# Second edge pass of a graph network: node sums over three edge tiles in two rounded matmul passes, run four steps behind instead of one

## The reference, cut to what matters

```python
x = layernorm(x + relu(gcn(x)))          # first layer: sums over edges into dst
# second layer, for each edge e = (i = src, j = dst):
xs, xv = x[:, :128] @ Ws, x[:, 128:] (128 x 3 values per node) @ Wv
s2, v2 = products of xs[j], xv[j] and the unit vector Y(e)
W  = (softplus-MLP of 20 edge features) * edge_weight
agg = segment_sum(concat(s2, v2) * W, i)
S, V = agg @ W1_s ..., agg @ W1_v @ W2_v
x = layernorm(x + concat(softplus(S) @ W2_s, V))
```

## Time and profile before

| | us |
|---|---|
| three runs, median (lowest, highest) | 1123.79 (1123.58, 1126.42) |
| the profiled execution, its own time | 1128.47 |
| its span in the profile | 1126.6 |
| PE busy, share of the span | 957.1 (85%) |
| DVE busy | 805.6 (72%) |
| ACT busy | 643.7 (57%) |
| POOL busy | 592.5 (53%) |
| mean granted TensorE clock | 0.897 of 2.4 GHz |

### The profile page before, as it was taken

How to read it: one execution, slowest core, us unless ns; L and a number is a source line. 1 busy time by engine, 2 the same in 40 slices (tenths; PEclk the granted TensorE clock), 3 DMA queues, 4 the chain that set the end, 5 groups by cost and what they waited for, 6 DMA issues and landing times.

```text
span 1126.6 us, 17245 instructions
## 1 busy us (share of the span) xinstructions
PE 957.1 (85%) x4727; PEld 739.9 (66%) x4727; DVE 805.6 (72%) x2527; ACT 643.7 (57%) x1460; POOL 592.5 (53%) x683
## 2 busy tenths in 40 slices
PE   6789999999848999999995699999999999444443
PEld 6768777877636888777774477777777777233332
DVE  7888877877716877877876466666666666278887
ACT  1169877877732555555555244445444444178887
POOL 3328888888742666666664456665665664300000
PEclk9979998999888999999998799999999999855555
DMA  9979999999995999999997588888888887599994
GB/s 353 419 249 233 246 241 238 259 240 246 224 235 178 307 324 316 311 313 313 313 315 265 170 184 202 194 204 205 194 201 205 197 198 150 101 354 363 368 347 169
DMA packets 152119, 285.77 MB, mean 254 GB/s; under 512 B 17690, under 2 KB 53950, under 8 KB 152030
## 3 DMA queue, kind: packets, MB, share of 16 engines
q1 hardware_dynamic: 103534, 191.44, 49.1%
q0 software_dynamic: 35392, 82.86, 37.0%
q10 hardware_dynamic: 13104, 10.43, 2.8%
HBM read 137.56 MB, written 147.10 MB: 253 GB/s over the span
## 4 chain that ended last, share of the span: by engine, by line
PE 37%; ACT 12%; issue 9%; DVE 8%; DMA 3%; ACTq 2%; POOL 1%; DVEq 0%; SPq 0%; POOLq 0%
PE bank L1175 6%; PE bank L1186 5%; PE bank L1143 4%; ACT node_mem L663 4%; DVE node_mem L916 3%; PE bank L1184 3%; PE bank L1200 3%; PE bank L1198 3%; PE bank L1201 3%; PE bank L1168 2%; ACT G_hi L646 2%; PE bank L1147 2%; PE bank L1182 2%; PE bank L1176 2%; ACTq L647 2%
## 5 line engine op out<-in xcount | busy, mean ns | idle before, releaser
L545 POOL DMA_INDIRECT sum<-R_mem,l_sidx x79 | 125.8, 1592 | 129.3 <-ACT R_mem L675 79.1
L489 POOL DMA_INDIRECT sum<-R_mem,sidx_all x79 | 128.9, 1632 | 73.2 <-DVE sidx_all L867 35.6
L520 POOL TENSOR_TENSOR node_mem<-node_mem,G_mem 128x512 f32<-128x512 f32 x75 | 96.9, 1292 | 87.9 <-ACT node_mem L657 87.8
L1143 PE MATMUL bank<-W0h,G_hi 128*128 128x512 f32 x316 | 132.3, 419 | 0.4 <-ACT G_hi L646 0.2
L1143 PE MATMUL bank<-W0l,G_hi 128*128 128x512 f32 x316 | 124.3, 393 | 0.0
L657 ACT ACTIVATE node_mem<-node_mem 128x512 f32<-128x512 f32 x75 | 47.5, 633 | 112.3 <-DVE node_mem L916 112.3
L965 DVE SCALAR_TENSOR_TENSOR edge_mem<-edge_mem,Y,bank 128x128 f32<-128x128 f32 x237 | 71.9, 387 | 49.8 <-ACT edge_mem L693 49.2
L693 ACT COPY edge_mem<-bank 128x256 f32<-128x256 f32 x79 | 29.4, 372 | 134.9 <-PE bank L1186 133.2
L1068 PE MATMUL bank<-G_hi,M_mem 128*128 128x512 f32 x200 | 89.0, 445 | 11.7 <-ACT R_mem L589 11.6
L1215 PE MATMUL bank<-ident,node_mem 128*128 128x128 f32 x80 | 27.5, 448 | 82.0 <-DVE node_mem L994 81.9
L537 POOL DMA_INDIRECT G_mem<-x_d,dst_i x79 | 78.3, 992 | 32.6 <-issue 30.7
(11 more groups left out here) (181 smaller groups left out, 2746.9 us busy)
## 6 DMA issues: line engine op xcount, KB each, us to landing
filt_d<-node_mem SPq DMA_DIRECT2D x40, 512.0 KB
G_mem<-x SPq DMA_DIRECT2D x79, 256.0 KB, 4.2
node_mem<-sum SPq DMA_DIRECT2D x79, 256.0 KB, 4.0
x_d<-node_mem SPq DMA_DIRECT2D x79, 256.0 KB, 2.5
node_mem<-filt_d SPq DMA_DIRECT2D x79, 256.0 KB
sum<-zeros SPq DMA_DIRECT2D x33, 512.0 KB
sum<-node_mem SPq DMA_DIRECT2D x79, 192.0 KB, 3.5
edge_mem<-sum SPq DMA_DIRECT2D x15, 512.0 KB, 5.2
```

The costliest lines, as they stand in the source:

```text
L489: pool.indirect_dma_start(sum0, bass.IndirectOffsetOnAxis(ap=sidx[:, t:t + 1], axis=0), R[t % 8][:, :], None, compute_op=ALU.add).then_inc ...
L520: pool.tensor_tensor(res[a], res[a], xl[a], ALU.add).then_inc(n_sum, 1)
L545: pool.indirect_dma_start(sum1, bass.IndirectOffsetOnAxis(ap=l1_sidx[:, t:t + 1], axis=0), R3[t % 8][:, :], None, compute_op=ALU.add).then ...
L1143: pe.matmul(bank[4 + a][:, :], zT_hi[a][:, c * P:(c + 1) * P], w[:, c, :], start=(c == 0 and w is W0h), stop=False)
```

## The change

Three tiles form a group now, where two did. For the tile with place j in its group there are j+1 blocks of the sum, of 128 sources each. The message times the edge's weight is split into two fp32r (rounded fp32) parts, `msg_hi` from ACT and `msg_lo` from DVE, each block is multiplied by both, and `M3` is 0/1 without the weight. So a group has 6 x 2 = 12 sum matmuls of fp32r operands; they accumulate in banks 4, 7 and 1 over three steps. The tile whose sums run in step s is s-10 (it was s-7), and they stand ahead of the second weights. The fifth transpose goes into columns 256 to 384 of `bank[5]`, since bank 1 now holds a sum. `us` runs in ACT's step s for tile s-7 (it was s-6). On DVE the messages, now those of tile s-7, come before the products of tile s-5. For tiles below 60 the trash rows are still counted in the first stage, with three index rows a step where there were four; for the last 19 DVE counts them in `edges1`.

```diff
-        M3 = ring("M3", 4, [P, 2 * P])
+        M3 = [[M_mem.rearrange("p a b -> p (a b)")[:, (6 * i + j * (j + 1) // 2) * P:(6 * i + (j + 1) * (j + 2) // 2) * P]
+               for j in range(3)] for i in range(3)]
+        msg_hi, msg_lo = G_hi, G_lo
...
+        sum_bank = (4, 7, 1)
...
 # SP
-                sp_.dma_start(trow3[g % 4][:, :], src_row[:, g * 256:(g + 1) * 256].broadcast_to([P, 256])) \
+                w = min(384, NP - g * 384)
+                sp_.dma_start(trow3[g % 4][:, 0:w], src_row[:, g * 384:g * 384 + w].broadcast_to([P, w])) \
...
 # POOL, r = g - 5
-                        pool.wait_ge(f_scat, 32 * r)
-                    for t in range(2 * r, min(2 * r + 2, TR)):
+                        pool.wait_ge(f_scat, 48 * r)
+                    if 3 * r >= LATE:
+                        pool.wait_ge(w_sidx, 2 + 2 * (r - T4 + 1))
+                    for t in range(3 * r, min(3 * r + 3, TR)):
...
 # ACT, e = s - 11
+                if live(s, 7):
+                    t, a = s - 7, (u - 7) % 4
+                    act.wait_ge(f_o, t + 1)
+                    wait(act, f_lo, t - 3)
+                    act.copy(msg[a][:, 0:256], bank[5][:, 0:256]).then_inc(f_us, 1)
                 if live(s, 4):
...
+                    act.copy(rawT[b][:, 512:640], bank[5][:, 256:384]).then_inc(f_rawT, 1)
                     act.copy(rawT[b][:, 0:512], bank[0][:, :]).then_inc(f_rawT, 1)
-                    act.copy(rawT[b][:, 512:640], bank[1][:, 0:P]).then_inc(f_rawT, 1)
+                if live(e, 0) and e % 3 == 2:
+                    for t in range(e - 2, e + 1):
+                        sums_out(t)
...
+                if live(s, 8):
+                    act.wait_ge(f_msg, K_MSG * (t + 1))
...
+                    act.activation(msg_hi[a][:, :], msg[a % 4][:, P:640], ACT.Identity, scale=ew[:, t:t + 1]).then_inc(f_hi, 1)
...
 # DVE, tm = s - 9
-                    dve.tensor_scalar(M3[c % 4][:, 0:w], trow3[r][:, 0:w], src_f[:, bass.ds(tm, 1)], ew[:, bass.ds(tm, 1)],
-                                      ALU.is_equal, ALU.mult).then_inc(f_M, 1)
+                    dve.tensor_scalar(M3[gm % 3][jm], trow3[gm % 4][:, 0:wm], src_f[:, tm:tm + 1], None, ALU.is_equal) \
+                       .then_inc(f_M, 1)
...
+                if live(s, 9):
+                    dve.wait_ge(f_hi, tm + 1)
+                    dve.scalar_tensor_tensor(msg_lo[tm % 8][:, :], msg[tm % 4][:, P:640], ew[:, tm:tm + 1],
+                                             msg_hi[tm % 8][:, :].bitcast(F32), ALU.mult, ALU.subtract).then_inc(f_lo, 1)
+                    if tm >= LATE:
...
+                        dve.scalar_tensor_tensor(trow[tm % 2][:, 0:wm], M3[gm % 3][jm].bitcast(F32), 1.0, before[:, Q - wm:Q],
+                                                 ALU.mult, ALU.mult, accum_out=l1_dup[:, tm:tm + 1]).then_inc(w_dup, 1)
+                        if jm == 2 or tm == TR - 1:
...
+                            sums_to(3 * gm, tm + 1, 2 + 2 * (gm - T4))
...
 # PE, the fifth transpose of tile t = s - 4, then the sums
-                    pe.transpose(bank[1][:, 0:P], G3[a][:, 0:C], ident[:, :]).then_inc(f_tr, 1)
+                    wait(pe, f_us, t - 2)
+                    pe.transpose(bank[5][:, 256:384], G3[a][:, 0:C], ident[:, :]).then_inc(f_tr, 1)
...
+                if live(s, 10):
+                    t = s - 10
+                    g, j = t // 3, t % 3
+                    last = j == 2 or t == TR - 1
+                    pe.wait_ge(f_lo, t + 1)
+                    pe.wait_ge(f_M, t + 1)
+                    for k in range(j + 1):
+                        if k == j:
+                            wait(pe, f_ev, 3 * g - 2 + k)
+                        for part_ in (msg_hi, msg_lo):
+                            ins = pe.matmul(bank[sum_bank[k]][:, :], M3[g % 3][j][:, k * P:(k + 1) * P], part_[t % 8][:, :],
...
                 if live(s, 6):
...
+                    pe.wait_ge(f_rawT, 2 * min(t + 2, TR - 1) + 1)
```

More of the change, by code:

```diff
@@ L25 @@
 NR = TR * P
+G1 = (TR + 2) // 3
+LATE = 3 * T4
 Q = 4 * P
@@ L304, in build @@
         f_msg = sem("f_msg")
+        f_hi = sem("f_hi")
+        f_lo = sem("f_lo")
         f_M = sem("f_M")
@@ L529, in _ @@
             pool.wait_ge(w_sidx, 2)
-            for g in range(T2 + 5):
-                if g < T2:
-                    for t in range(2 * g, min(2 * g + 2, TR)):
+            for g in range(G1 + 5):
+                if g < G1:
+                    for t in range(3 * g, min(3 * g + 3, TR)):
                         if t >= 8:
@@ L669, in edges1, with sums_out @@
             def edges1(s, u):
[L670 to L682, removed]
+                e = s - 11
+                def sums_out(t):
+                    act.wait_ge(f_mm, t + 1)
+                    wait(act, f_scat, 48 * (t // 3 - 1))
+                    act.copy(R3[t % 8][:, :], bank[sum_bank[t % 3]][:, :]).then_inc(f_ev, 1)
+                if live(s, 7):
[3 more added lines that the diff above has]
+                    act.copy(msg[a][:, 0:256], bank[5][:, 0:256]).then_inc(f_us, 1)
                 if live(s, 4):
@@ L701, in edges1 @@
                                    scale=Y[:, bass.ds(t, 1), 0]).then_inc(f_proj0, 1)
-            for s in range(TR + 8):
+            for s in range(TR + 11):
                 edges1(s, s % 8)
@@ L820, in counts1 @@
                     if s >= 1:
[L821 to L826, removed]
+                        dve.wait_ge(w_dup, 3 * s)
+                    for v in range(3):
+                        t, w = 3 * s + v, (v + 1) * P
+                        dve.scalar_tensor_tensor(junk1[v][:, 0:w], bank[3][:, 0:w], src_f[:, t:t + 1], before[:, Q - w:Q],
+                                                 ALU.is_equal, ALU.mult, accum_out=l1_dup[:, t:t + 1]).then_inc(w_dup, 1)
                 if s >= 1:
@@ L944, in edges1 @@
                                                      ALU.mult, ALU.add))
+                if live(s, 7):
+                    t, c = s - 7, (u - 7) % 4
+                    dve.wait_ge(f_us, t + 1)
+                    st = Stage(f_msg, t, K_MSG)
+                    mo = msg[c][:, 256:640].rearrange("p (c i) -> p c i", i=3)
+                    for i in range(3):
+                        st.mark(dve.scalar_tensor_tensor(mo[:, :, i], msg[c][:, 0:P], Y[:, bass.ds(t, 1), i],
+                                                         bank[6][:, i * P:(i + 1) * P], ALU.mult, ALU.add))
                 if live(s, 5):
@@ L1047, in _, with index_rows @@
             pe.wait_ge(s_wTc, 3)
[L1049 to L1051 removed]
+            def index_rows(cols, to, g, n=4):
+                for v in range(n):
+                    t = n * g + v
                     ins = pe.transpose(to[:, v * P:(v + 1) * P], cols[:, t:t + 1].broadcast_to([P, P]), ident[:, :])
@@ L1176, in edges1 @@
                     pe.matmul(bank[3][:, 0:P], Wins[:, :], rawT[b][:, 512:640], start=True, stop=True).then_inc(f_wv, 1)
+                if live(s, 10):
[9 more added lines that the diff above has]
+                            ins = pe.matmul(bank[sum_bank[k]][:, :], M3[g % 3][j][:, k * P:(k + 1) * P], part_[t % 8][:, :],
+                                            start=(k == j and part_ is msg_hi), stop=(last and part_ is msg_lo))
+                        if last:
+                            ins.then_inc(f_mm, 1)
                 if live(s, 6):
@@ L1188, in edges1 @@
                     ins.then_inc(f_o, 1)
[L1189 to L1200, removed]
-                        pe.matmul(bank[7][:, :], M3[a][:, P:2 * P], msg[a][:, P:640], start=True, stop=True).then_inc(f_mm, 1)
-            for s in range(TR + 7):
+            for s in range(TR + 10):
                 edges1(s, s % 8)
```

63 lines of the change are left out of this document (31 added, 32 removed).

## The result

| | before | after |
|---|---|---|
| median of four runs, us | 1124.20 | 1136.98 |
| lowest, highest | 1123.58, 1126.42 | 1136.08, 1139.16 |
| profiled execution, its span | 1126.6 | 1137.4 |

The ratio is 1.0101, 95% interval [1.0083, 1.0119]: 12.8 us slower. The forecast was 1135.8 us, 12.0 slower.

What follows compares the result with a forecast made beforehand. PE's array time was taken to bound the second edge pass; steady steps +6.9, beginning -3.7, steps 83 and 84 +1.3, way out +7.5, index rows +0.5 and first pass -0.5 gave +12.0, 1135.8 us, range 1119 to 1149.

Steps and rivals of the forecast that it cites:

- The pause at the fifth transpose: Second edge pass: PE's fifth transpose waits for ACT's `us` copy from the same bank, 0.29 us in every step.
- A: PE's five transposes in a step: 0.55 us before, forecast to end 0.84 after the previous second weights.
- The pause at the bank: Second edge pass: a group's first sum waits until ACT empties bank 4, 0.51 us once in three steps.
- B: PE's first weights in a step: 1.08 us, forecast to end 1.92 after the previous second weights.
- The three kinds of step: Second edge pass: steps with two, four and six sum matmuls take 4.23, 4.19 and 4.65 us, mean 4.36.
- ACT and DVE at nothing: Second edge pass: ACT (4.22 us in its longest step) and DVE (3.6 a step) keep PE's pace, costing nothing.
- The beginning and steps 83 and 84: Second edge pass: steps 7 to 9 without sums save 3.7 us; the last two steps cost 1.3 more.
- The way out: From the last second weights to the last stage's loads: scatter-add rounds take 24.1 us, not 16.6, +7.5.
- First edge pass and index rows: Fewer index transposes and counts in the first edge pass, -0.5 us; more first index rows ahead of the gathers, +0.5.
- No pauses: Rival, second edge pass: PE's waits are covered, a step takes 3.90 us, total 1101; chance 0.15.
- Only one pause: Rival, second edge pass: only `us` is waited for; PE steps 3.72, 4.19, 4.65, ACT gives 0.3 back, 1129; chance 0.14.
- The clock did not fall: Rival, second edge pass: PE's pauses lower its granted clock to 0.93, +21 us, total 1157; chance 0.10.

Runs made afterwards that it cites:

- the second pair: The kernel before and the changed kernel, both unaltered, run again on one other chip: 1128.71 and 1142.69 us, ratio 1.0107.
- both edits: Changed kernel with the fifth transpose moved to bank 3 and ACT's copy of the group's first sum moved ahead of `us`: 1107.74 us, 0.978 of before.
- the second experiment: Changed kernel with only ACT's copy of the group's first sum moved ahead of `us`: 0.9965 of before.

## Why the prediction was right

- **What bounds.** PE's array time, with pauses added to it. Right: with the pauses taken away one at a time the steps fell by 0.24 each and 0.57 once in three, with both by 1.32 for three, and half the sum matmuls brought 1.25 to 1.35.
- **The pause at the fifth transpose.** Forecast A = 0.84, measured 0.79. The handover from PE to ACT (0.20) and the copy (0.37) were as in the earlier trace rows; the restart was over-priced. I took 0.16 beyond the array time from a 512-column fp32r matmul; at this transpose it is 784.23 - 784.01 - 0.11 = 0.11.
- **The pause at the bank.** Forecast PE's restart at 2.43 after the last second weights, measured 790.74 - 0.23 - 788.06 = 2.45. Its removal brought 0.57 of a step, where 0.51 stood, because A was shorter and so B ended sooner. That the restart came out to 0.02 hides two errors: the copy ended at 2.23 and not 2.27 (789.69, 0.60 long), and PE's restart behind it took 0.22 and not the 0.16 of the earlier trace rows.
- **The three kinds of step.** Forecast 4.23, 4.19, 4.65; measured 4.25, 4.16, 4.62. Per step +0.07 instead of +0.095, hence +4.8 instead of +6.9 over 73 steps.
- **ACT and DVE at nothing.** Right in the changed kernel: PE's waits for DVE are 0.7 us in all from 640 to 975 us. ACT's step with three sums ends so that `us` begins 0.20 after the second weights each time.
- **The beginning and steps 83 and 84.** -3.7 and +1.3 forecast, -3.9 (-2.9 in the second pair) and +1.1 measured.
- **The way out** is the term that was mis-sized: +7.5 forecast, +10.0 and +11.3 measured. The mechanism was right, three rounds from about the end of the last second weights. But the round of 72 to 74 started at +2.5 and not +1.3, since the landing before it took 4.51, and the two landings that I put at 3.8 and 3.77, the shorter of those in the earlier trace rows, took 4.62 and 4.28. With 5.0, the other row, the sum would have been nearer. The upper bound of the tail, +3 or 10.5 in all, held the first measurement and was passed by 0.8 in the second.
- **First edge pass and index rows.** -0.5 and +0.5 forecast; the start of the pass moved by -1.7 in one pair of traces and by 0.0 in the other, and the spread between traces is larger than either term, so neither is confirmed. The second is also not what its source gives: 0.25 MB at 292 GB/s are 0.9 us.
- **The rivals.** "No pauses" (1101) did not occur in the changed kernel, but describes the kernel with both edits, whose way out (23.6) is near the 24.1 that the rival took: 0.978 x 1124.2 is 1099.5. "Only one pause" has the steps of the second experiment (3.72, 4.19 and 4.65 for 3.68, 4.15 and 4.62), but neither ACT's 0.3 nor the way out of 24.1 came, so 1120.3 and not 1129. DVE did not set the pace. The clock did not fall: 1.00 from 660 to 965 us with two kinds of pause in it. By the Trainium skill, page TensorE: Matmul & The Clock Gate, section on PSUM-queue depth-cycling, it could have swung; pauses of 0.24 and 0.57 us did not bring that about here. The sum matmuls of 512 columns keep the array for 0.23 each (785.56 to 785.79, and 3.90 a step without gaps bears it out). The 131 ns that the same page of the Trainium skill gives, in its section "Back-to-back issue gap", found no support here; the measured 0.23 decides.

That the total was met to 1.2 us is in part luck. Two errors of opposite sign nearly cancel, 2.1 to 2.5 us too much for the steps and 2.5 to 3.8 too little for the way out, and the two pairs of traces themselves differ by 2.6 (10.8 and 13.4 between the spans).

## What to carry to other kernels

When work is moved away from between a result and the next use of its buffer, write down for each engine what now lies over the handover, in us: here 0.44 of transposes over a handover of 0.68 (0.20, the copy's 0.37, 0.11), where at least 0.86 of sums had lain over it as well. Look for a free piece of another bank and for the place of the copy in the other engine's list before giving up the saving; two small edits turned +1.0% into -2.2%. And price the drain by itself: a chain of transfers that wait for one another is hidden in the steady pass and bare at its end. Larger groups lengthened it here by 10 to 11 us, and an earlier copy out of the first bank, which lets each round start earlier, took 3 to 4 back.

## What the runs showed that I had not expected

- The restart after a wait costs less for a 128-column transpose (0.11 from the end of ACT's copy beyond the array time) than for a 512-column fp32r matmul (0.16 in the earlier trace rows, 0.22 at the bank in the second edge pass).
- The list of waits can miss a pause: PE shows none at L1203 although each costs 0.24, since the modelled end of the matmul before covers it. The distance between starts shows it, and so does the weight load.
- The landing of a round of scatter-adds took between 3.4 and 6.7 us at the end of the pass in these traces. In every kernel SP issues eight row loads near the first of these rounds, and the longest landings (6.71, 6.00, and 5.00 in the earlier trace rows) are beside them, but so are some of 3.7, 4.2 and 4.5. What makes the difference was not tried.
- DVE could be busy 90% of the time (238.64 of 265 us) with PE never waiting for it in that stretch.
- Where ACT empties the group's first bank changes more than the step: the way out was 23.0 to 23.6 us with the early copy and 26.6 to 27.7 with the late one.
